# Re-spacing LayerNorm, output-projection and DMA work in a fused fp32 decoder block

## The reference

```python
def reference(x, ctx_2048, ...):
    x = x + _L0_attn_ref(_layernorm(x), q_w, q_b, k_w, k_b, v_w, v_b, o_w, o_b)   # causal self-attention
    x = x + _L0_xattn_ref(_layernorm(x), ctx_2048, ctx_2048)                      # causal, keys = values = ctx
    x = x + _L0_ffn_ref(_layernorm(x), W_up, W_down, W_gate, W_expert)
    return x

def _L0_ffn_ref(x, W_up, W_down, W_gate, W_expert):
    logits = x @ W_gate.T
    routing_weights, _ = top_k(logits, 2)
    shared_out = relu(x @ W_up.T) @ W_down.T
    rw = softmax(routing_weights, axis=-1)
    return shared_out + sum(rw, axis=-1, keepdims=True) * (x @ W_expert)
```

## Time and profile before

| | |
|---|---|
| median of 3 runs | 722.88 us (722.45 to 724.98) |
| the profiled execution | 724.98 us, span 723.1 us |
| PE busy | 680.8 us, 94% |
| DVE busy | 501.2 us, 69% |
| ACT busy | 501.0 us, 69% |
| POOL busy | 257.9 us, 36% |
| chain that ended last, by engine | PE 77%, DVE 11%, ACT 5%, DMA 3%, issue 2%, POOL 1% |
| granted TensorE clock, mean | 0.986 |

### The profile page before, as it was taken

How to read it: one execution, slowest core, us unless ns; L and a number is a source line. 1 busy time by engine, 2 the same in 40 slices (tenths; PEclk the granted TensorE clock), 3 DMA queues, 4 the chain that set the end, 5 groups by cost and what they waited for, 6 DMA issues and landing times.

```text
span 723.1 us, 13877 instructions
## 1 busy us (share of the span) xinstructions
PE 680.8 (94%) x4488; PEld 524.9 (73%) x4488; DVE 501.2 (69%) x1730; ACT 501.0 (69%) x1450; POOL 257.9 (36%) x391
## 2 busy tenths in 40 slices
PE   7998999999999999999987997999989999899998
PEld 6776777767787677777665774777768777577786
DVE  6658766666766776777787689867897669564632
ACT  5678877667876778788796888666687657774110
POOL 4745544333564335732355434433221012000100
PEclk9999999999999999999987999999999999999999
DMA  9753423336423473444676776544364444510101
GB/s 315 180 147 85 128 67 88 88 102 166 116 62 82 124 207 85 96 112 115 177 212 139 188 178 181 139 110 103 79 173 101 110 95 104 145 45 1 58 1 58
DMA packets 52326, 86.12 MB, mean 119 GB/s; under 512 B 8608, under 2 KB 16800, under 8 KB 52256
## 3 DMA queue, kind: packets, MB, share of 16 engines
q1 hardware_dynamic: 52256, 85.25, 45.3%
HBM read 27.55 MB, written 7.34 MB: 48 GB/s over the span
## 4 chain that ended last, share of the span: by engine, by line
PE 77%; DVE 11%; ACT 5%; DMA 3%; issue 2%; POOL 1%; SPq 1%; ACTq 0%; POOLq 0%; DVEq 0%
PE t L483 14%; PE m L522 14%; PE m L523 13%; PE m L524 13%; PE pv L516 9%; PE s L469 8%; DVE probs L683 4%; ACT probs L911 2%; DMA stack<-stage 2%; DVE xT_lo L769 1%; DVE prob L693 1%; PE m L483 1%; DMA xres<-in_x 1%; ACT prob L920 1%; DVE f_xln L746 1%
## 5 line engine op out<-in xcount | busy, mean ns | idle before, releaser
L683 DVE CUSTOM_DVE_ANT_0 probs<-s,mask 128x128 f32<-128x128 f32 (+3 forms) x512 | 245.8, 482 | 137.6 <-PE s L469 135.2
L911 ACT ACTIVATE probs<-probs,negmax 128x128 f32<-128x128 f32 (+3 forms) x512 | 284.7, 559 | 45.2 <-DVE negmax L683 44.0
L483 PE MATMUL t<-ident,probs 128*128 128x128 f32 x1134 | 203.1, 277 | 11.1 <-POOL probs L1024 4.8
L469 PE MATMUL s<-stack 96*128 96x128 f32 (+3 forms) x512 | 200.3, 397 | 5.5 <-DVE negmax L683 3.8
L920 ACT ACTIVATE prob<-t 128x512 f32<-128x512 f32 (+1 forms) x236 | 126.3, 537 | 110.4 <-PE t L483 110.2
L1024 POOL TENSOR_SCALAR probs<-probs,rsum 128x128 f32<-128x128 f32 (+3 forms) x256 | 133.4, 539 | 189.2 <-DVE rsum L697 189.2
L483 PEld LDWEIGHTS t<-ident,probs 128*128 128x128 f32 x1134 | 144.0, 142 | 60.5 <-issue 10.7
L469 PEld LDWEIGHTS s<-stack 96*128 96x128 f32 x512 | 98.8, 193 | 19.3 <-DVE negmax L683 4.3
L911 ACT ACTIVATION_READ_ACCUMULATOR probs<-probs,negmax 128x1 f32 x512 | 99.0, 193 | 0.0
L693 DVE COPY prob<-t 128x128 f32<-128x128 f32 (+1 forms) x210 | 73.8, 351 | 31.8 <-PE t L483 30.9
L522 PE MATMUL m<-xT_hi,w_lo 128*128 128x512 f32 x192 | 78.5, 409 | 1.5 <-DVE xT_lo L751 1.2
(11 more groups left out here) (144 smaller groups left out, 961.5 us busy)
## 6 DMA issues: line engine op xcount, KB each, us to landing
stack<-stage SPq DMA_DIRECT2D x384, 128.0 KB, 2.3
xt<-in_x SPq DMA_DIRECT2D x16, 256.0 KB, 4.3
xres<-in_x SPq DMA_DIRECT2D x4, 1024.0 KB, 6.0
kraw<-in_ctxT SPq DMA_DIRECT2D x16, 256.0 KB, 3.0
cv<-in_ctx SPq DMA_DIRECT2D x16, 256.0 KB, 3.2
x<-xres SPq DMA_DIRECT2D x3, 1024.0 KB, 4.6
res<-x SPq DMA_DIRECT2D x8, 256.0 KB, 5.5
out<-res SPq DMA_DIRECT2D x2, 1024.0 KB, 4.8
```

The source lines that it names most:

```text
L469: nc.tensor.matmul(score_tile(P, i), stack[0:RS, P % 2, h, 0, chunk(qb)], stack[0:RS, P % 2, h, 1, 0:N], start=True, stop=True).then_inc(s ...
L483: mm = nc.tensor.transpose(dst[:, chunk(qb - kb)], probs[:, (2 * P + h) % 3, OFF[qb] + PART * kb:OFF[qb] + PART * kb + PART], ident[:, :])
L683: nc.vector.tensor_tensor_reduce(probs[:, (2 * P + h) % 3, OFF[qb]:OFF[qb + 1]], score_tile(P, i), mask[:, T - N:T], -SCALE, BIG, ALU.add, ...
L911: nc.scalar.activation(tile, tile, ACT.Exp, bias=negmax[:, P % 2, h, qb:qb + 1], scale=-1.0, accum_out=total).then_inc(p_exp, 1)
```

## The change

The same arithmetic is done by the same instructions on the same engines. What moves:

- **LayerNorm slots.** j = 5: statistics from (34,0), (34,0), (34,1), (34,1) to (32,1), (32,5), (33,1), (33,5); normalisations from (36,0), (36,0), (36,1), (36,1) to (35,4), (35,5), (36,0), (36,1). j = 7: statistics from (48,0), (48,0), (48,1), (48,1) to (47,1), (47,5), (48,1), (48,5), normalisations from (52,0), (52,0), (52,1), (52,1) to (51,4), (51,5), (52,0), (52,1). j = 6: normalisations from (44,0), (44,0), (44,1), (44,1) to (44,0), (44,1), (44,4), (44,5). The feed-forward normalisations go from two in slot 0 and two in slot 1 to one in each of slots 0 to 3.
- **Projections.** O(2,3) from (31,4) to (29,4), O(3,3) from (40,0) to (39,4). Q, K and FL hold their bank no longer by one slot.
- **Residual exchange of batch 3.** Store from step 33 to 30, load from 34 to 31, `biased(3, t)` from steps 34 to 37 to two each in steps 32 and 33. The load of res1 goes from step 32 to 30, that of res2 from 41 to 40, the DOWN weight from 44 to 43 and its split from steps 46, 47 to 45, 46.
- **TensorE.** One wait for all four `scaled` instructions of a head in place of four.
- **VectorE.** The low part of FL is made in the same slot as ScalarE's high part, one slot earlier; `context_lo` in slot 4 in place of 5.
- **ScalarE.** `context_hi` stands behind the exponential and the copy of its slot.
- **GpSimd.** `scaled(s+1, 0)` is the last thing of a step; `ln_scale` is a step later for all but j = 6.

```diff
-    return [z + 16, z + 16, z + 17, z + 17] if j == B + 1 else [z, z, z + 1, z + 1]
+    return [z + 1, z + 5, z + 9, z + 13] if j == B + 1 else [z - 7, z - 3, z + 1, z + 5]
...
-    return [z + 32, z + 32, z + 33, z + 33]
+    if j == B + 2:
+        return [z + 32, z + 33, z + 36, z + 37]
+    return [z + 28, z + 29, z + 32, z + 33]
...
-    return [z, z, z + 1, z + 1]
+    return [z, z + 1, z + 2, z + 3]
...
-        put(("Q", n), 2 * G - 4, 4 if n and n % KC == 0 else 0, 4, 1)
-        put(("K", n), 2 * G - 3, 0, 4, 1)
+        put(("Q", n), 2 * G - 4, 4 if n and n % KC == 0 else 0, 4)
+        put(("K", n), 2 * G - 3, 0, 4)
...
-                put(("O", b, t), SELF_END + t, 0, 4)
+                put(("O", b, t), SELF_END + min(t, 2), 4 * (t // 3), 4)
             elif b == B - 2:
-                put(("O", b, t), (25, 28, 29, 31)[t], 4 * (t // 3), 4)
+                put(("O", b, t), (25, 28, 29, 29)[t], 4 * (t // 3), 4)
...
-                for n in range(1, B):
-                    first = PAIRS * n + 5 if n < B - 1 else NPS + 1
-                    if s == first:
-                        sp.wait_ge(o_out, NT * n)
-                        sp.dma_start(x2[n - 1], xres[:, :, :]).then_inc(x2_stored[n - 1], 16)
-                    if s == first + 1:
-                        sp.wait_ge(x2_stored[n - 1], 16)
-                        sp.dma_start(xres[:, :, :], x_in[n]).then_inc(res_loaded, 16)
+                if p == 5 + b // 3 and 1 <= b < B:
+                    sp.wait_ge(o_out, NT * b)
+                    sp.dma_start(x2[b - 1], xres[:, :, :]).then_inc(x2_stored[b - 1], 16)
+                if p == 6 + b // 3 and 1 <= b < B:
+                    sp.wait_ge(x2_stored[b - 1], 16)
+                    sp.dma_start(xres[:, :, :], x_in[b]).then_inc(res_loaded, 16)
...
-                if s == 32:
+                if s == 30:
                     sp.wait_ge(o_mm, NT * 3)
...
-                if s == SELF_END + 4:
                     sp.wait_ge(o_mm, NT * B)
                     sp.wait_ge(x2_stored[2], 16)
                     load_x(res2, x2[2])
-                if s == SELF_END + 7:
+                if s == SELF_END + 6:
...
-                if kb == 0 and not own(P // 2):
-                    pe.wait_ge(p_exp, PAIRS * P + NT * (h + 1))
+                if kb == 0:
+                    if own(P // 2):
+                        pe.wait_ge(p_done, PAIRS * own_rank(P) + NT * (h + 1))
+                    else:
+                        pe.wait_ge(p_exp, PAIRS * P + NT * (h + 1))
...
-                    if kb == 0 and own(P // 2):
-                        pe.wait_ge(p_done, PAIRS * own_rank(P) + NT * h + qb + 1)
...
-                        if key[0] in ("Q", "K", "FL"):
+                        if key[0] in ("Q", "K"):
                             empty(key)
...
-                    if s % 2 == 0 and own(s // 2 - 1) and i == 5:
+                    if s % 2 == 0 and own(s // 2 - 1) and i == 4:
                         context_lo(s // 2 - 1)
...
+                if s % 2 == 1 and other((s - 3) // 2):
+                    added((s - 3) // 2)
                 if s % 2 == 0 and other(s // 2 + 2):
                     keys(s // 2 + 2)
-                if own((s + 1) // 2):
-                    for qb in range(NT):
-                        scaled(s + 1, 0, qb)
...
-                    if s == stats_slots(j)[-1] // PAIRS:
+                    if s == stats_slots(j)[-1] // PAIRS + (j != B + 2):
                         ln_scale(j)
...
-                    if s == NPS + 2 + t:
+                    if s == NPS + t // 2:
                         biased(B - 1, t)
...
+                if own((s + 1) // 2):
+                    for qb in range(NT):
+                        scaled(s + 1, 0, qb)
```

32 lines of the change are left out of this document (13 added, 19 removed).

## The result

| | before | after |
|---|---|---|
| median | 723.63 us (722.45 to 724.98) | 730.98 us (729.90 to 731.96) |
| profiled execution's span | 723.1 us | 729.1 us |
| PE busy | 680.8 us | 678.7 us |

A forecast was written before the change was run, and what follows sets the result against it. TensorE was taken as busy for 680.8 of 723.1 us, with late engines setting the time in a dozen places. Gains and costs summed to +0.4 on the median of 722.88: 723.3 us, range 716.4 to 731.0.

The forecast's parts named there:

- bank holds: L(2,1) and L(3,1) get a bank that K has just left, as in step 3: +0.6 us, each between nothing and 1.0.
- feed-forward's norms: Feed-forward normalisations only change places with score blocks on a full VectorE: nothing.
- exchange and O(2,3): Step 35: GpSimd's wait for the residual's load goes, -3.2 us; O(2,3) in step 29 lets step 33 start earlier, +0.2.
- low part of FL: Steps 43, 51 and 60: made one slot earlier, TensorE's gate waits shrink by 0.8, 0.7 and 0.6 us: -2.1.
- O(3,3) with res2: O(3,3) costs 3.0 us in step 39, two thirds taken back in step 40: +1.0, bounds -0.5 and +2.6.
- LN slots j = 5, j = 7: Normalisations between score blocks, step 35 +1.2 us and step 51 +0.5; j = 5 statistics in steps 32 and 33 +0.5.
- single wait, context's low half: Three transposes can't start early in two or three heads where GpSimd is late, +0.4 us; context parts nothing.
- GpSimd's order: Step 24: bias and memset stand ahead of pair 25's first head, TensorE waits: +1.8 us, bounds 0 and 2.1.
- clock and DMA: Shorter waits may keep the clock up, transfers moved out of steps 32 to 34: -0.5 us, bounds +1 and -4.
- Rival B: VectorE and ScalarE set the time from step 29 to 52; work leaving values bursts costs fully: 731.0 us, 0.30 with milder forms.
- Rival C: The load of xres is still not in time, so the -3.2 is gone: 726.5 us, chance 0.06.
- Rival A: The exchange was key, costs are hidden; step 35 falls to 7.5 us: 716.4 us, chance 0.22 with weaker forms.

## Why the prediction was wrong

The sum was +0.4, measured +8.0. What failed are three terms: the bank holds were priced at 0.6 us and cost 3.5, the feed-forward's norms were put at nothing and cost 2.5, and the early load of the DOWN weight, which has no term at all, cost up to 3.2. Set against each other by ratio, each part at the value in the company that is nearest to the change (uncertain by 2 to 3 us each):

| term | forecast | measured |
|---|---|---|
| exchange and O(2,3) | -3.0 | -3.7 |
| low part of FL | -2.1 | -2.0 |
| O(3,3) with res2 | +1.0 | +1.3 |
| LN slots j = 5, j = 7 | +2.2 | +0.4 with the exchange |
| single wait, context's low half | +0.4 | -0.1 (steps 24, 27 and 28: +1.2) |
| ScalarE's order | 0 | +0.4 |
| GpSimd's order | +1.8 | +2.3 with the exchange, +5.5 alone |
| bank holds | +0.6 | +3.5 |
| feed-forward's norms | 0 | +2.5 in the change, +3.1 alone, +0.3 with both gains |
| DOWN weight in SyncE's queue | not costed | +3.2 in the change, +1.2 alone |
| clock and DMA | -0.5 | not separable (it is in the terms above) |

The measured column adds up to 7.8 of 8.0. That it comes so close is luck: ten values uncertain by 2 us make a sum uncertain by about 6, the norms and the DOWN weight overlap, and with every part at its value alone the column adds up to 8.5. The stronger evidence is the changed kernel with three parts undone. There holds, GpSimd's order and DOWN weight together are worth 9.3 us (+-2.6) where the table has 9.0, and what is left of the change gains 1.3 where the table has 1.2. So the theory of separate waits stands in the main, with the reserve that three of the costs depend on what else is changed.

**Right.** The exchange: -3.7 by ratio, and what came late next was, as written, GpSimd's first head behind the scale of j = 5 (2.96 us of wait at 384.47, for the head that GpSimd scales in the last place of step 34). The step that the sum started from, 12.17 us, was near the upper end of what this step takes; by profiles alone the gain could be anything from 1 to over 5 us. The FL step in its direction: the low part one slot earlier at three gates. The waits shrank by 0.37 each, not 0.6 to 0.8, and the steps by 0.6, 0.5 and 0.4, 1.5 us together. The rest of the -2.0 is the clock in step 60, which the prediction had in another term; that the forecast -2.1 was met is partly luck. Step 25: +1.70. O(3,3): two thirds came back alone (1.69 of 2.55 in step 40), about half in the change (1.20). That steps 32 to 34 would change by under 2 us together: they changed by 0.5.

**Failed steps.** (1) *"The same constellation in step 3 made TensorE wait 0.32 us"*. The wait without a hold was 1.25 us at each of two places, and it grew the step by 0.95, the upper end of what was allowed for one. But the term also named only these two places. The rule without a hold holds for all Q and K, and what takes the freed bank next is not only an L but any group of turned probabilities: that is where steps 26 and 27 grew. (2) *"The feed-forward ones only change places with score blocks on a full VectorE: nothing."* The argument that gave the norms of j = 5 a price, two of four taken out of the slots beside the values burst, held here too and was not applied. It was the wrong way round: the norms that were priced (1.2 + 0.5 + 0.5) cost 0.4, and the ones at nothing 2.5, with intervals of over 2 us about each. A full engine does not make order free, because TensorE waits for one particular result. (3) *The DOWN load was left out*, though SyncE was listed as an engine whose queue runs in order. One row of SyncE's waits shows that the load was already 1.9 us early at the old place, so that it would wait for about a step more at the new one, with the next stack behind it. It was: SyncE waited 13.7 us and TensorE 2.44 us for that stack at 477.18. (4) *Rival B* came to the measured time, 731.0, by coincidence, with another sum: it charged O(2,3), the norms of j = 5 and 7 and the statistics in full, which cost little, and nothing for the holds and SyncE. Its condition, VectorE and ScalarE as the bound from step 29 on, is not what was found: four of the waits lie at single operands, two of them in steps 11 and 19. *Rival C* fell: no wait for xres in the change after step 33. *Rival A* was right on the exchange and FL, and the kernel that keeps only these two is faster than both.

**The rule that was weighed.** By the Trainium skill, "SBUF — State Buffer", section "Who interferes with whom", the norms moved to step 35 might also push GpSimd's head back, at a further 1.3 us. The part cost 0.4 us with the exchange, and GpSimd's two heads of pair 35 took 2.07 us each in the change and 2.05 before: both were done when the first moved norm began. The instruction that the norm did meet, the cast of the keys (L1053), took 0.84 us, where it takes about 0.61 in fourteen of its sixteen places:

```profile
389.53 0.54 DVE L738 TENSOR_SCALAR V<-res,mv,rstd 128x512 f32<-128x512 f32 x1
```

```profile
389.70 0.84 POOL L1053 CAST stage<-kraw 128x512 fp32r<-128x512 f32 x1
```

The next norm, at 390.93, took 1.26 us beside GpSimd's L1055. So the trace agrees with the page in both directions. It did before, too: the head at 291.45 took 2.39 us in place of 2.05, with norms of VectorE from 290.98 and from 292.49 beside it, and the prediction's "no case of the other direction" misread the trace.

## What to carry to other kernels

For each operation that is moved, list every queue that it sits in, what it waits for at the new place, and who stands behind it; a load that waits for a buffer blocks all loads behind it, at a price that can rise as the other engines get earlier. Where a rule changes for a class (a hold for all of a kind), count all its users and all who take the freed resource, not the two places at hand. And run the parts one by one: of eleven here two gained, and they alone gave -5.9 us.
